# Differential attention with a gated output on one core: P and the heads turned by DMA, and the product with V ahead of the projections

## The reference, cut to what matters

```python
xn = layernorm(x)
q, k, v = split(xn @ Wqkv.T + bqkv)         # v: [.., 4, 256], used by two query pairs each
p1 = softmax(causal(q[..., 0] @ k[..., 0].T / sqrt(128)))
p2 = softmax(causal(q[..., 1] @ k[..., 1].T / sqrt(128)))
p = p1 - lam * p2
o = p @ v                                    # 256 columns for each of 8 pairs
o = o * rsqrt(mean(o * o) + 1e-5) * subln_w * (1 - lambda_init)
s = o.reshape(.., 2048) @ out_w.T + out_b
g = silu(mxfp4(xn) @ mxfp4(ffn_w).T + ffn_b) # 4-bit values with a shared scale for each 32
out = x + s * g
```

## Time and profile before

| | |
|---|---|
| median of 3 runs | 1835.9 us |
| profiled execution | 1837.28 us, its span 1835.5 us |
| TensorE, VectorE, ScalarE, GpSimd busy | 1678.7, 1269.1, 964.5, 710.0 us |
| TensorE clock granted, mean over the span | 0.977 |
| instructions | 29927 |
| DMA | 42.04 MB, mean 23 GB/s |

### The profile page before, as it was taken

The page is one execution under the profiler, slowest core; times in us unless marked ns, Lnnn a source line. Parts: engine busy times, 40 slices in busy tenths (PEclk is TensorE's granted clock), DMA queues, the critical chain, the costliest instruction groups (busy, mean ns, idle before and its releaser), DMA issues.

```text
span 1835.5 us, 29927 instructions
## 1 busy us (share of the span) xinstructions
PE 1678.7 (91%) x10545; PEld 1039.1 (57%) x10577; DVE 1269.1 (69%) x2829; ACT 964.5 (53%) x2642; POOL 710.0 (39%) x1442
## 2 busy tenths in 40 slices
PE   3568999999899999999999999999989999999988
PEld 2345565556655565556655566555655566556654
DVE  4668888548874688648884588646885488845772
ACT  4554566436653566436664366534664366634661
POOL 2214553226422463225532364224632255323243
PEclk7879999999999999999999999999999999999999
DMA  7300000100000000100001000010001000000001
GB/s 258 92 24 1 1 1 1 52 18 1 1 30 30 12 1 1 41 24 7 1 4 49 18 2 1 29 35 7 1 1 41 24 7 1 7 24 24 1 1 40
DMA packets 20680, 42.04 MB, mean 23 GB/s; under 512 B 1682, under 2 KB 2228, under 8 KB 20532
## 3 DMA queue, kind: packets, MB, share of 16 engines
q1 hardware_dynamic: 20532, 40.13, 6.5%
HBM read 31.74 MB, written 8.39 MB: 22 GB/s over the span
## 4 chain that ended last, share of the span: by engine, by line
PE 37%; DVE 28%; ACT 15%; issue 12%; POOL 6%; DMA 0%; SPq 0%; POOLq 0%; DVEq 0%; ACTq 0%
PE ps L418 11%; PE ps L420 10%; PE ps L419 10%; ACT pp L654 9%; DVE negmax L922 6%; DVE pp L937 4%; DVE qkv L879 4%; DVE ps L920 2%; DVE coef L935 2%; DVE ebias L925 1%; ACT qkv L632 1%; PE ps L542 1%; PE ps L474 1%; DVE v L889 1%; PE ps L476 1%
## 5 line engine op out<-in xcount | busy, mean ns | idle before, releaser
L654 ACT ACTIVATE pp<-ps,ebias,ssc 128x384 f32<-128x384 f32 (+3 forms) x512 | 312.1, 614 | 289.2 <-DVE ebias L925 229.7
L418 PE MATMUL ps<-xT,wqkv 128*128 128x512 f16 x768 | 295.2, 384 | 8.5 <-DVE qkv L879 5.3
L419 PE MATMUL ps<-xT,wqkv 128*128 128x512 f16 x768 | 294.4, 383 | 0.0
L420 PE MATMUL ps<-xT,wqkv 128*128 128x512 f16 x768 | 294.3, 383 | 0.0
L700 ACT ACTIVATE junk<-ps 128x256 bf16<-128x256 f32 x256 | 98.0, 383 | 270.4 <-PE ps L420 270.3
L418 PE MATMUL ps<-qkv,pT 128*128 128x256 f16 x640 | 175.2, 274 | 56.8 <-issue 41.0
L922 DVE TENSOR_REDUCE negmax<-ps 128x2 f32<-128x256 f32 (+3 forms) x256 | 211.1, 824 | 8.8
L911 DVE SCALAR_TENSOR_TENSOR res<-ps,small,obias 128x512 f32<-128x512 f32 x32 | 24.0, 751 | 249.0 <-PE ps L420 249.0
L418 PE MATMUL ps<-wout,heads 128*128 128x512 f16 x512 | 194.0, 379 | 0.0
L419 PE MATMUL ps<-wout,heads 128*128 128x512 f16 x512 | 194.0, 379 | 0.0
L420 PE MATMUL ps<-wout,heads 128*128 128x512 f16 x512 | 194.0, 379 | 0.0
(11 more groups left out here) (150 smaller groups left out, 3768.0 us busy)
## 6 DMA issues: line engine op xcount, KB each, us to landing
xin<-in_L_attn_hidden_states SPq DMA_DIRECT2D x8, 1024.0 KB, 5.3
xres<-in_L_attn_hidden_states SPq DMA_DIRECT2D x32, 256.0 KB, 2.8
out_x<-res SPq DMA_DIRECT2D x32, 256.0 KB, 2.0
qkv<-in_L_attn_Wqkv_w SPq DMA_DIRECT2D x8, 512.0 KB, 9.7
heads<-in_L_attn_Wqkv_w SPq DMA_DIRECT2D x8, 512.0 KB, 11.5
qkv<-in_L_attn_out_w SPq DMA_DIRECT2D x4, 512.0 KB, 3.8
heads<-in_L_attn_out_w SPq DMA_DIRECT2D x4, 512.0 KB, 3.6
gate<-in_L_ffn_weight SPq DMA_DIRECT2D x1, 1024.0 KB, 13.2
```

Of the source, the lines that this page charges most:

```text
L418: mm(out, ah, bh, start=start and j == 0, stop=False)
L419: mm(out, ah, bl, start=False, stop=False)
L420: last = mm(out, al, bh, start=False, stop=stop and j == n - 1)
L654: run(pp[:, m, 0:w], sc_ps[:, m, 0:w], ACT.Exp, bias=ebias[:, m:m + 1], scale=ssc[:, c:c + 1], accum_out=psum_l[:, s % 2, m:m + 1]).then_i ...
```

## The change

The attention steps are rewritten as a deeper pipeline, and the turns leave TensorE.

- P is rounded before it is turned: ScalarE writes the high half of `pp` to `ph` (`p_hi`), VectorE the low half (`p_lo`), and SyncE issues one DMA transpose that turns both halves, 128 x 2w float16, into `pT`. The normalised head is likewise written as two halves (`normalised`, `normalised_lo`) and turned by a second DMA into `oT`, one for each step.
- The banks that held the turned tiles now hold a second pair of score banks, so scores are made two steps ahead.
- The second map's exponential is written back to its score bank, not to SBUF.
- Mask, maximum and scale are one VectorE instruction for each map (`maxima(n, m)`), which is followed by a read-out; ScalarE starts on the second map while the first map's maximum is still to come.
- TensorE's list in step n is: scores of n+2, attend of n, fills of n. The product with V stood behind the fills before.
- VectorE's is: combination of n+1, maximum of n+2 (second map), low half of P of n+1, maximum of n+2 (first map), low half of the head of n-1, fills of n. ScalarE's is: square of n-1, high half of P of n+1, head of n-1, exponentials of n+2, fills of n.
- SyncE's list now has two turns in each step, and between them the loads of x and of the residual and the stores of the output.
- A step's number is a plain count over all 256 steps (`place`), and each fill carries its counts (`plan`).

The core of the diff:

```diff
-            def transpose_o(s, step):
...
-            def attend(g, s, step):
-                i = s // 2
-                wait(pe, pT_hi, step + 1)
-                wait(pe, pT_lo, step + 1)
-
-                wait(pe, on_done, step - 1)
+            def attend(n):
+                b, g, r, w = place(n)
+                i, u = r // 2, n % 2
+                if r in (0, 4):
+                    pe.wait_ge(v_lo, 8 * b + 2 * g + (1 if r == 0 else 2))
+                pe.wait_ge(pT_done[u], 16 * (n // 2 + 1))
+
+                wait(pe, on_lo, n - 1)
...
+            for n in range(NSTEPS):
+                b, s = n // NS, n % NS
+                if n + 2 < NSTEPS:
+                    scores(n + 2)
+                attend(n)
+                for f in PLAN[n]:
...
+                    fill(f)
...
+            def transpose_p(n):
+                w = place(n)[3]
+                wait(sp, ph_lo, n + 1)
+                wait(sp, pv_done, n - 1)
+                sp.dma_start_transpose(pT[:, n % 2, 0:2 * w // P, :], ph[:, n % 2, 0:2 * w])\
+                  .then_inc(pT_done[n % 2], 16)
+
+            def transpose_o(n):
...
+                wait(sp, on_lo, n + 1)
+                if b and g == 0:
+
+                    sp.wait_ge(fill_done, fill_of("out", b, 0, i) + 1)
...
+                if n + 1 < NSTEPS:
+                    transpose_p(n + 1)
+                if n:
+                    transpose_o(n - 1)
...
+            def exps(n):
+                u, w = n % 2, place(n)[3]
+
+                wait(act, l2_done, n - 3)
+                for a, m in enumerate((1, 0)):
+                    act.wait_ge(max_done, 2 * n + a + 1)
+                    sc = sc_ps[u][:, m, 0:w]
+                    if m == 0:
+
+                        wait(act, ph_lo, n)
+                    run(sc if m else pp[:, 0:w], sc, ACT.Exp, bias=ebias[:, u, m:m + 1], scale=-1.0,
+                        accum_out=psum_l[:, n % 4, m:m + 1]).then_inc(exp_done, 1)
...
+            for n in range(NSTEPS):
+                if n:
+                    square_o(n - 1)
+                if n + 1 < NSTEPS:
+                    p_hi(n + 1)
+                if n:
+                    normalised(n - 1)
+                if n + 2 < NSTEPS:
+                    exps(n + 2)
+                for f in PLAN[n]:
+                    fill(f)
...
+            def maxima(n, m):
...
+                nc.vector.tensor_tensor_reduce(sc, sc, mask[:, S - w:S], ssc[:, c:c + 1], BIG, ALU.add, ALU.min,
+                                               ebias[:, u, m:m + 1]).then_inc(max_done, 1)
...
+                if n + 1 < NSTEPS:
+                    combine(n + 1)
+                if n + 2 < NSTEPS:
+                    maxima(n + 2, 1)
+                if n + 1 < NSTEPS:
+                    p_lo(n + 1)
+                if n + 2 < NSTEPS:
+                    maxima(n + 2, 0)
+                prepare_some(b, s, 0)
+                if n:
+                    normalised_lo(n - 1)
+                prepare_some(b, s, 1)
+                for f in PLAN[n]:
+                    fill(f)
+                prepare_some(b, s, 2)
```

More of the change, by code:

```diff
@@ L1 @@
 import math
+from collections import namedtuple
 from contextlib import ExitStack
@@ L108, with plan, place, fill_of @@
 PROLOGUE = [("xT", 0, k) for k in range(NT)] + [(kind, 0, j) for kind, j in PROJ]
[L109 to L113, removed]
+Fill = namedtuple("Fill", "kind g j n hi v ffn gate out")
+def plan():
+    n = hi = v = ffn = 0
+    rows = []
+    for b in range(-1, B):
+        steps = schedule(b > 0, b < B - 1) if b >= 0 else [PROLOGUE]
+        for step in steps:
+            row = []
+            for kind, g, j in step:
+                gate = 4 * b + j
+                out = 4 * b + (j if kind == "last" else j - NT)
+                row.append(Fill(kind, g, j, n, hi, v, ffn, gate, out))
+                n += 1
+                hi += kind in ("q", "k", "xT")
+                v += kind == "v"
+                ffn += kind == "ffn"
+            rows.append(row)
+    return rows[0], rows[1:], n
+FIRST, PLAN, FILLS = plan()
+assert len(FIRST) % 2 == 0
+END = [Fill("out", 0, k, FILLS + k - (NT - 2), 0, 0, 0, 0, (B - 1) * NT + k) for k in (NT - 2, NT - 1)]
+NSTEPS = B * NS
+def place(n):
+    return n // NS, n % NS // STEPS, n % STEPS, (n % STEPS // 2 + 1) * P
+def fill_of(kind, b, g, j):
+    rows = [FIRST, *PLAN]
+    lo = max(0, b * NS + 1 - (NS // 4 if g == 0 and kind in ("q", "k", "v", "xT") else 0) - (2 if kind == "xT" else 0))
+    for row in rows[lo:lo + NS + NS // 4]:
+        for f in row:
+            if (f.kind, f.g, f.j) == (kind, g, j):
+                return f.n
+    raise KeyError((kind, b, g, j))
 WB = 2 * NC * G
@@ L130, in setup_order @@
             i += 1
[L131 to L157, removed]
+    return order + [("fill", m) for m in range(i, len(PROLOGUE))] + [("scores", 0)] + [("o", n) for n in range(OB)] \
+        + [("ahead", 0)]
 def build(nc, x_d, wqkv_d, bqkv_d, lq1_d, lk1_d, lq2_d, lk2_d, sub_d, ow_d, ob_d, fw_d, fb_d, out_d):
@@ L407, in _ @@
+            transpose_o(NSTEPS - 1)
+            for k in range(1, NT):
+                if k > 1:
+                    residual(B - 1, k)
+                store(B - 1, k)
             sp.wait_ge(res_free, 16 + 16 * B * NT)
@@ L584, in _ @@
+            for f in END:
+                fill(f)
         @block.scalar
@@ L1032, in _ @@
+            normalised_lo(NSTEPS - 1)
+            for f in END:
+                fill(f)
         @block.gpsimd
@@ L1163, in _, with gating @@
-            batches(pool, body)
-            n = len(PROLOGUE) + FILLS_0 + (B - 2) * FILLS_B + len(sum(schedule(True, False), []))
-            for k in (NT - 2, NT - 1):
-                finish(k, (B - 1) * NT + k, n + 1)
-                n += 1
+            def gating(f):
+                pool.wait_ge(tanh_done, f.gate + 1)
+                pt(t2, t2, one.broadcast_to([P, HID]), ALU.add).then_inc(tanh_one, 1)
+                pool.wait_ge(tanh_one, f.gate + 1)
+                pt(gate[:, f.j, :], t2, gate[:, f.j, :], ALU.mult).then_inc(gate_done, 1)
@@ L1170 @@
+            norm_of(NSTEPS - 1)
+            for f in [*PLAN[NSTEPS - 1], *END]:
+                if f.kind == "out" or f.kind == "last" and LAST_PIECES[f.j][f.g][1] == OC:
+                    finish(f)
 _INS = ["L0_attn_hidden_states", "L0_attn_Wqkv_w", "L0_attn_Wqkv_b", "L0_attn_lambda_q1", "L0_attn_lambda_k1",
```

536 lines of the change are left out of this document (229 added, 307 removed).

## The result

The changed kernel takes 1950.24 us (median of 4 runs, 1947.59 to 1957.75) against 1835.97 of the kernel before on the same chip: ratio 1.0632, 95% interval 1.0601 to 1.0663. The forecast was 1870: the sign was right, the size was not, 114 us more where 34 were forecast. The profiled execution took 1957.75 us, its span 1954.7.

A forecast was written before the change was run, and what follows sets the result against it. TensorE was taken to bound each batch's first quarter, a VectorE-ScalarE loop the rest. Quarters of -1.0, -0.4, +2.2 and +2.6 us gave +27 over eight batches, start and end +7: 1870 us, range 1790 to 2010.

The forecast's parts named there:

- What bounds the kernel: TensorE bounds a batch's first quarter (79.60 of 79.60 us busy); a loop between VectorE and ScalarE bounds the other three.
- 109 us off TensorE: 1152 turns of P and heads leave TensorE; only the first quarter gains, at most 4.7 us a batch.
- Loop A: One-step round of VectorE and ScalarE in light steps: 4.96 us; eight steps come to 39.5 against 39.1 before.
- rival 3: The turn is short (2.0 us) and the kernel gets faster: 1801 us, second quarter 45; chance 0.31.
- Loop B: Two-step loop through DMA turn, product with V, projection and fills: 7.37 us plus the turn; longer once the turn exceeds 2.5.
- L = 2.8: Time of one DMA turn in us, taken from a 256 KB load; 2.0 and 5.3 were the ends.
- Fused maximum in one pass: VectorE's fused mask and maximum costs one pass (0.545 us); the rival of two passes gave 1938 us, chance 0.08.
- its conflict with VectorE passes moves from the combination to P low, at nothing: GpSimd's conflict with VectorE passes shifts to the low rounding of P and adds no time.
- their sharing at nothing: Two turns a step, and transfers of x, residual and output, share SyncE's queue at no cost.
- The clock: TensorE matmuls of 512 columns were all priced at 0.215 us, with no term for a slower clock.
- Second quarter, 47.2: Eight light steps 41.7 us, gate work 4.3 and two rounding operations 1.2: 47.2 against 47.6 before.
- the long turn (L = 4): Rival: a DMA turn takes 4 us or more, giving 2019 us at 4 and 2180 at 5.3; chance 0.15.

The follow-up runs named there:

- hot_pe: Changed kernel with idle 256-column matmuls, output never read, between scores and product with V in 16 of 32 steps of batches 1 to 7: 1908.74 us.

## Why the prediction was wrong in size

Point by point, by its own steps:

- *What bounds the kernel; 109 us off TensorE; only the first quarter can cash it in*: right. With the order undone that quarter is 74.8 us in batch 4 and 74.3 in the mean, where 74.9 were counted.
- *Loop A, 4.96 us; gives nothing back*: nearly. In the kernel with the product last the light steps of the fourth quarter are 42.4 us for eight, where 39.5 and 3.6 of roundings made 43.1. The second quarter is not met so well: 47.7 where rival 3 has 45.
- *Loop B and L = 2.8*: right as a mechanism; that the numbers agree so closely is in part luck. Of the signs that were named, the turns land in 2.7 us, TensorE is busy 1613 us and waits 1.0 us in the mean in front of each product of the last three quarters. The slope was 124 us for each microsecond and about 127 was measured, and quarters 3 and 4 came within 0.6 us (45.2 and 45.9 for 45.5 and 45.3), but half clock, which the sum left out, is in all of these: with it nearly gone (hot_pe) the third quarter is 43.2 us.
- *Fused maximum in one pass*: right.
- *"its conflict with VectorE passes moves from the combination to P low, at nothing"*: this step failed. The new two-input coefficient, which the prediction priced like the old one (0.29 us), met the conflict and took 1.25. The four waits behind the output projections were forecast at 0.5, 0.1, 2.1 and 1.0 us and measured (mean of batches 1 to 6, steps 3, 5, 7 and 9) 1.1, 0.9, 3.2 and 1.9: 0.6 to 1.1 more each, 3.4 a batch, where the coefficient is 0.96 longer than priced in each of these steps and lies on the chain. No run takes both blocks away with the product in front, so this price is read from the chain; by experiment, with the block passed on to the low half, 15 us came back.
- *"their sharing at nothing"* (transfers and turns on one queue): failed at one place. The two turns a step did not get in each other's way on the queue: each issue holds it for 1.2 us, where under half a microsecond was taken from plain transfers, yet every turn of P was issued within 0.48 us of its low half. But the load of x and that of the residual stand beside the turn of step 1, and the product that needs it waits 3.8 us, a wait that the sum didn't have; moving the loads gave 20 us. The other 1.9 us of that wait stay with the loads moved. The coefficient of step 1 is blocked too in every batch from 1 on, but no run shows how much of the 1.9 that is.
- *The clock*: the sum took 0.215 us for every matmul of 512 columns. The waits it forecast itself were short, but those that came, of some 3 us and more, were followed by half clock. This term was put at nothing without a reason; 41 us by experiment.
- *Second quarter, 47.2*: 51.1 in the mean, 48.3 in the best batch. Step 9's wait falls in it (the sum had it in the first), and in some batches single turns of 4 to 5 us (57.1 in batch 3, 52.6 in batch 5). What makes these late is open: beside the longest of them, 5.10 us in step 13 of batch 3 and 4.94 in step 15 of batch 5, no load or store was under way. And since the quarter is 2.7 us above its sum with the product last too, where no turn is waited for, a part of the miss may be in the terms for the gate and the roundings.

Together 13.3 us a batch: 9.0 in the first quarter, that is 5.4 of waits (9.1 in steps 1 to 7 against 3.7), 3.1 of half clock by the estimate of above, and a rest of 0.5; 3.9 in the second; and 0.3 for the last two. The prediction had the right loops and the right L, and took for free three things that the wait then exposed. The experiments should not be added as terms (15, 20 and 41 us): a shorter wait was also followed by less half clock, and no run combines them with the product in front. Of the rivals none happened: the long turn (L = 4) is out by the rows, the short one too. What the prediction did not ask is what the pipeline would do with the product left at the end of the list, which was worth more than all its terms.

## What to carry to other kernels

When an operand comes late by a latency that no engine works on, put the instruction that waits for it behind all the independent work of its queue: here the same turns cost some 127 us for each microsecond in front of the projections, and nothing behind them. When an edit gives a VectorE instruction a second input in SBUF, however small, look for the GpSimd pass beside it. What helped here was an operand in PSUM (43 long passes, then none), not another form of one instruction, which passed the block on. And price a wait of TensorE of some microseconds with the slower matmuls behind it.

## What was not expected of the hardware

- A VectorE operation of one column lasted 1.25 us beside a GpSimd pass of 1.26 us; taken away, the block passed to the next instruction with two SBUF inputs.
- A DMA turn of 64 KB lands 2.4 us after its input is ready and one of 256 KB 3.35 us: four times the bytes for 0.95 us. Its issue holds SyncE's queue for 1.2 us at the median, against 0.40 to 0.57 for the loads of x and the residual and the stores.
- A turn of 64 KB took 5.03 us with a 1 MB and a 256 KB load under way, 2.41 without.
- Matmuls without use in the waits of TensorE made the kernel 41 us faster.
